# Eight plain gathers ahead of the stored table, joint gathers at most three in flight, and one written-out fill in an attention factorization machine on one core

## What is computed

```python
V = emb_v[x]                                  # (32, 2048, 64)
iu, ju = np.triu_indices(F, k=1)              # 496 pairs
VV = V[iu] * V[ju]
hid = jax.nn.relu(jnp.einsum('pbk,kh->pbh', VV, at_w) + at_b)
score = jnp.einsum('pbh,ho->pbo', hid, at_h)
pooled = jnp.sum(VV * score, axis=0)
at_fm_score = pooled @ p
fm1 = w0 + jnp.sum(w1[x], axis=0)
prob = jax.nn.sigmoid(at_fm_score + fm1)
```

## Time and profile before

| what | value |
|---|---|
| median of 3 runs | 842.64 us (840.57 to 845.03) |
| the profiled execution | 840.11 us, span 838.3 us |
| PE busy | 785.2 us, 94% of the span |
| DVE busy | 721.5 us, 86% |
| ACT busy | 640.2 us, 76% |
| POOL busy | 568.4 us, 68% |
| gathers' share of the 16 DMA engines | 47.1% |

### The profile page before, as it was taken

The page is one execution under the profiler, slowest core; times in us unless marked ns, Lnnn a source line. Parts: engine busy times, 40 slices in busy tenths (PEclk is TensorE's granted clock), DMA queues, the critical chain, the costliest instruction groups (busy, mean ns, idle before and its releaser), DMA issues.

```text
span 838.3 us, 26331 instructions
## 1 busy us (share of the span) xinstructions
PE 785.2 (94%) x10550; PEld 278.0 (33%) x10550; DVE 721.5 (86%) x1221; ACT 640.2 (76%) x672; POOL 568.4 (68%) x553
## 2 busy tenths in 40 slices
PE   0448999999999999999999999999999999999998
PEld 0113333333333333333333333333333333333332
DVE  2473989899999999999999999999999999999884
ACT  0245778788887878888888788898888888888775
POOL 6727767666677666667676666676766667767772
PEclk9878999999999999999999999999999999999999
DMA  9975859635423446543243448823443435833300
GB/s 182 149 47 22 26 23 25 24 23 22 24 21 23 22 21 22 22 22 24 20 24 22 22 21 22 23 22 22 23 23 21 22 21 23 24 21 23 12 1 1
DMA packets 19910, 24.27 MB, mean 29 GB/s; under 512 B 10472, under 2 KB 10541, under 8 KB 19885
## 3 DMA queue, kind: packets, MB, share of 16 engines
q0 software_dynamic: 17408, 17.07, 47.1%
q1 hardware_dynamic: 1535, 6.64, 2.1%
q10 hardware_dynamic: 942, 0.22, 0.1%
HBM read 20.59 MB, written 3.31 MB: 29 GB/s over the span
## 4 chain that ended last, share of the span: by engine, by line
PE 91%; issue 2%; POOL 2%; DMA 2%; ACT 2%; DVE 1%; ACTq 0%
PE Z L580 55%; PE SG L596 27%; PE SG L610 5%; PE Z L544 4%; POOL rows L296 2%; DMA rows<-in_L_rec_emb_v_dram,idx 2%; ACT H L520 1%; ACT pV L465 1%; DVE X L439 0%; DMA idx_raw<-in_r_x_dram 0%; PE Z L674 0%; PE SG L556 0%; ACT V L454 0%; PE Z L653 0%; ACT y_sb L530 0%
## 5 line engine op out<-in xcount | busy, mean ns | idle before, releaser
L439 DVE TENSOR_TENSOR X<-V 128x992 f32<-128x992 f32 (+15 forms) x1024 | 634.8, 691 | 32.5 <-ACT V L454 18.4
L296 POOL DMA_INDIRECT rows<-table,joint_idx x480 | 500.6, 1043 | 232.5 <-issue 153.8
L520 ACT ACTIVATE H<-Z,bias 128x1024 f32<-128x1024 f32 x512 | 529.3, 1119 | 122.8 <-PE Z L580 119.3
L580 PE MATMUL Z<-X,w_sb 64*64 64x512 f32 x4096 | 479.8, 602 | 14.7 <-issue 10.0
L580 PEld LDWEIGHTS Z<-X,w_sb 64*64 64x64 f32 x4096 | 148.2, 132 | 296.3 <-issue 289.3
L596 PE MATMUL SG<-H,score_w 128*32 128x512 f32 x2048 | 239.5, 597 | 0.0
L596 PEld LDWEIGHTS SG<-H,score_w 128*32 128x32 f32 x2048 | 56.8, 109 | 173.7 <-issue 96.1
L465 ACT ACTIVATE pV<-V,pmask 128x1024 f32<-128x1024 f32 x64 | 81.4, 1276 | 0.1
L407 DVE TENSOR_TENSOR prod<-SG,gram 128x512 f32<-128x512 f32 x32 | 22.1, 691 | 61.8 <-PE SG L596 61.8
L454 ACT COPY V<-Z 128x1024 f32<-128x1024 f32 x31 | 31.4, 1012 | 34.7 <-PE Z L544 34.7
L610 PEld LDWEIGHTS SG<-V,pV 128*32 128x32 f32 x4096 | 42.5, 109 | 23.5 <-issue 18.8
(11 more groups left out here) (46 smaller groups left out, 34.5 us busy)
## 6 DMA issues: line engine op xcount, KB each, us to landing
rows<-table,joint_idx POOLq DMA_INDIRECT x480
table<-joined SPq DMA_DIRECT2D x4, 792.0 KB
H<-in_L_rec_emb_v_dram SPq DMA_DIRECT2D x4, 768.0 KB, 8.6
rows<-in_L_rec_emb_v_dram,idx POOLq DMA_INDIRECT x32, 9.0
w_all<-in_L_rec_w_dram,idx POOLq DMA_INDIRECT x32
idx_raw<-in_r_x_dram SPq DMA_DIRECT2D x2, 64.0 KB, 2.0
idx_raw<-in_r_x_dram ACTq DMA_DIRECT2D x2, 64.0 KB, 2.2
table<-tail SPq DMA_DIRECT2D x1, 54.7 KB
```

The lines of the kernel that those rows point to most:

```text
L296: pool.indirect_dma_start(out=rows[t % 2][:, g * FILL_M + m, half, c0:c1], out_offset=None, in_=source, in_offset=bass.IndirectOffsetOnAxi ...
L439: last_one = nc.vector.tensor_tensor(xo, vj, vi.unsqueeze(3).to_broadcast(shape), ALU.mult)
L520: nc.scalar.activation(H[:, s % H_SLOTS, :, COLS * g:COLS * g + COLS], Z[:, z_slot(t, r), :, :], ACT.Relu, bias=bias[:, 0:1]).then_inc(hid ...
L580: done = nc.tensor.matmul(Z[64 * par:64 * par + 64, z_slot(t, r), half, :], w_sb[k, :], X[k, s % X_SLOTS, par, COLS * g:COLS * g + COLS], ...
```

## The change

- Only group 0 of fill 0 is gathered plain (8 gathers instead of 32). Group 1 of fill 0 and all later fills are joint, so they stand behind the wait for the table.
- Every joint gather from fill 1's fourth on waits until the gather three before it has landed. Four semaphores, `rows_landed0` to `rows_landed3`, are used in turn, so that each counts one gather at a time. PE waits for all four ahead of a turn.
- The turn stands ahead of round 6 in every fill that has one in its rounds, but for fill 0, whose order is its own.
- Only fill 0 is written out; the loop begins at fill 1.
- ACT copies `w1` values for fills 0 (group 1) and 1 too; 8 small `w1` gathers are left at the end instead of 32.

```diff
-TURN_BEFORE, LATE_TURN = 6, 12
-LATE_FILLS = (1, 2)
+TURN_BEFORE = 6
...
-PLAIN_FILLS = 2
 TAIL = (VOCAB - MAIN) // TAIL_RUN
 GROUP_AFTER = (0, 3, 7, 10)
+LANES, IN_FLIGHT = 4, 3
...
-def turn_before(t):
-
-    return LATE_TURN if isinstance(t, int) and t in LATE_FILLS else TURN_BEFORE
-
-
-def z_slot(t, r):
-
-    return (r if r < turn_before(t) else r + 1) % Z_SLOTS
+def z_slot(r):
+
+    return (r if r < TURN_BEFORE else r + 1) % Z_SLOTS
...
-        second_rows = sem("second_rows")
-        rows_gathered = [sem(f"rows_gathered{i}") for i in range(2)]
+        rows_landed = [sem(f"rows_landed{lane}") for lane in range(LANES)]
...
         def over_fills(eng, fill):
 
             fill(0, 0, True, False)
-            fill(1, 1, False, False)
-            fill(2, 0, False, False)
-            with eng.Fori(3, FILLS - 2, 2) as t:
+            with eng.Fori(1, FILLS - 2, 2) as t:
                 fill(t, 1, False, False)
                 fill(t + 1, 0, False, False)
             fill(FILLS - 1, (FILLS - 1) % 2, False, True)
...
-            def gather(t, paced=False):
-
-                joint = t >= PLAIN_FILLS
-                source, at_rows = (flat, joint_idx) if joint else (emb_v, idx)
-                for g in range(2):
+            def gather(t, groups=(0, 1), paced=False):
+
+                for g in groups:
+                    joint = t > 0 or g > 0
+                    source, at_rows = (flat, joint_idx) if joint else (emb_v, idx)
                     for m in range(FILL_M):
                         if paced and g == 0 and m == 0:
                             pool.wait_ge(gram_ready, t - 1)
                         elif paced and m % 2 == 0:
                             pool.wait_ge(z_ready, ROUNDS * (t - 2) + GROUP_AFTER[2 * g + m // 2])
                         for half in range(2):
+                            n = GATHERS * (t - 1) + 2 * (FILL_M * g + m) + half
+                            if n >= IN_FLIGHT:
+                                pool.wait_ge(rows_landed[(n - IN_FLIGHT) % LANES], 16 * ((n - IN_FLIGHT) // LANES + 1))
                             col = (2 * half + g) * NM + t * FILL_M + m
                             c0, c1 = (0, ROW) if joint else (EMB_AT[half], EMB_AT[half] + EMB)
-                            arrived = first_rows[g] if t == 0 else second_rows if t == 1 else rows_gathered[t % 2]
+                            arrived = first_rows[g] if t == 0 else rows_landed[n % LANES]
                             pool.indirect_dma_start(out=rows[t % 2][:, g * FILL_M + m, half, c0:c1], out_offset=None,
                                                     in_=source,
                                                     in_offset=bass.IndirectOffsetOnAxis(ap=at_rows[:, col:col + 1], axis=0)
                                                     ).then_inc(arrived, 16)
 
-            plain_w1 = [(Q, n) for n in range(PLAIN_FILLS * FILL_M) for Q in range(QUARTERS)]
+            plain_w1 = [(2 * half, n) for half in range(2) for n in range(FILL_M)]
...
             pool.wait_ge(idx_ready, 1)
-            gather(0)
-            pool.wait_ge(idx_ready, 2)
-            gather(1)
+            gather(0, groups=(0,))
             pool.wait_ge(idx_ready, 4)
             pool.wait_ge(table_stored, 16 * (PIECES + 1))
+            gather(0, groups=(1,))
+            gather(1)
             pool.wait_ge(first_turned, 2)
+            pool.wait_ge(w1_kept, 2)
             gather(2)
             for t in range(3, FILLS):
                 pool.wait_ge(rows_turned, t - 2)
-                pool.wait_ge(w1_kept, 2 * (t - 1 - PLAIN_FILLS))
+                pool.wait_ge(w1_kept, 2 * (t - 1))
                 gather(t, paced=True)
             for Q, n in plain_w1:
                 gather_w1(Q, n)
...
+                g0 = 1 if isinstance(t, int) and t == 0 else 0
                 for half in range(2):
-                    src = rows[parity][:, :, half, W1_AT[half]].rearrange("p (g m) -> p g m", g=2)
-                    nc.scalar.copy(w1_all[:, 2 * half:2 * half + 2, bass.ds(t * FILL_M, FILL_M)], src
+                    src = rows[parity][:, :, half, W1_AT[half]].rearrange("p (g m) -> p g m", g=2)[:, g0:2, :]
+                    nc.scalar.copy(w1_all[:, 2 * half + g0:2 * half + 2, bass.ds(t * FILL_M, FILL_M)], src
                                    ).then_inc(w1_kept, 1)
...
-                        late = turn_before(t) == LATE_TURN
-                        if r == turn_before(t):
+                        if r == TURN_BEFORE:
                             keep_v(t + 1, 1 - parity)
-                        if r == (14 if late else 12):
+                        if r == 12:
                             keep_pv(t + 1, 1 - parity, 0)
                             keep_w1(t + 1, 1 - parity)
-                        if r == (15 if late else 14):
+                        if r == 14:
...
+                        keep_w1(0, 0)
...
                 if first:
                     keep_v(1, 1)
                     for half in range(2):
                         keep_pv(1, 1, half)
+                    keep_w1(1, 1)
...
-                if isinstance(t, int) and t == 1:
-                    pe.wait_ge(second_rows, 16 * GATHERS)
-                else:
-                    pe.wait_ge(rows_gathered[parity], gathered(t, parity))
+                for lane in range(LANES):
+                    pe.wait_ge(rows_landed[lane], 16 * GATHERS // LANES * t)
+                pe.nop(nofuse=True)
...
-                    if r == turn_before(t) and not first and not last:
-                        pe.wait_ge(hid_ready, ROUNDS * t + turn_before(t) - Z_SLOTS + 1)
+                    if r == TURN_BEFORE and not first and not last:
+                        pe.wait_ge(hid_ready, ROUNDS * t + TURN_BEFORE - Z_SLOTS + 1)
                         turn(t + 1, 1 - parity)
...
-                pe.wait_ge(w1_first, 16 * QUARTERS * PLAIN_FILLS * FILL_M)
-                pe.wait_ge(w1_kept, 2 * (FILLS - PLAIN_FILLS))
+                pe.wait_ge(w1_first, 16 * 2 * FILL_M)
+                pe.wait_ge(w1_kept, 2 * FILLS)
                 pe.wait_ge(hid_ready, ROUNDS * FILLS)
...
             products(0, 0, True, False)
-            products(1, 1, False, False)
-            products(2, 0, False, False)
-            products(3, 1, False, False, head)
-            with pe.Fori(3, FILLS - 2, 2) as t:
+            products(1, 1, False, False, head)
+            with pe.Fori(1, FILLS - 2, 2) as t:
                 products(t, 1, False, False, rest)
                 products(t + 1, 0, False, False)
                 products(t + 2, 1, False, False, head)
```

More of the change, by code:

```diff
@@ L92, in z_before @@
         return r - 2
-    return r - 2 if turn_before(t) <= r < turn_before(t) + 2 else r - 3
+    return r - 2 if TURN_BEFORE <= r < TURN_BEFORE + 2 else r - 3
 def afm_kernel(nc, r_x, emb_v, at_w, at_b, at_h, p, w0, w1, out):
@@ L519, in relus @@
                         act.wait_ge(scored, STEPS * t + s - H_SLOTS + 1)
[L520 removed]
+                    nc.scalar.activation(H[:, s % H_SLOTS, :, COLS * g:COLS * g + COLS], Z[:, z_slot(r), :, :], ACT.Relu,
                                          bias=bias[:, 0:1]).then_inc(hid_ready, 1)
@@ L569, in hidden @@
                 pe.wait_ge(x_ready, ROUNDS * t + r + 1)
-                if r == turn_before(t) + 2 and not first and not last:
+                if r == TURN_BEFORE + 2 and not first and not last:
                     pe.wait_ge(v_ready, t + 1)
                 elif not first or r >= Z_SLOTS:
-                    pe.wait_ge(hid_ready, ROUNDS * t + z_before(t, r) + 1)
+                    pe.wait_ge(hid_ready, ROUNDS * t + z_before(r) + 1)
                 pe.nop(nofuse=True)
@@ L579, in hidden @@
                     for par in range(2):
-                        done = nc.tensor.matmul(Z[64 * par:64 * par + 64, z_slot(t, r), half, :], w_sb[k, :],
+                        done = nc.tensor.matmul(Z[64 * par:64 * par + 64, z_slot(r), half, :], w_sb[k, :],
                                                 X[k, s % X_SLOTS, par, COLS * g:COLS * g + COLS], start=True, stop=True)
```

5 lines of the change are left out of this document (1 added, 4 removed).

## The result

The changed kernel took **888.98 us** at the median of its four runs (873.7, 881.0, 896.95 and 908.95), beside 841.84 for the kernel before on the same chip, 5.6% more. Executions more than 1.5% above a kernel's quickest count as slow and are left out of every ratio here, so the ratio of 1.042, 95% interval 1.033 to 1.051, rests on the two quickest runs alone. It is slower, and even the quickest run lies above the range of 835 to 859. The profiled execution is that quickest one, 873.7 us; its span of 871.8 us is **33.5 us** longer than the 838.3 of before.

What follows compares the result with a forecast made beforehand. TensorE's own work was taken as the bound, 24.08 us a fill. Terms +1.3 (start), -0.2 (loop), +1.3 (middle), -0.5 (end) sum to +1.9, on the median of 842.64 giving 844.5 us, range 835 to 859.

Steps and rivals of the forecast that it cites:

- Steps 1 and 2: Start: table stored by 32 us instead of 64; first joint gather at 32.8, fill 2's last rows landing at 90.1.
- the pace of 1.41: Gather stream: with three in flight, one gather every 1.41 us, with ends 1.25 and 1.60.
- Rival A: Gather stream: the cap doesn't bind, POOL keeps its own pace, 4.6 us go; 837.5 us, chance 0.26.
- Step 3: PE through fills 0 and 1: waits 8.6 us for fill 2's rows; fill 2's grams at 108.5, +1.3 us.
- The stop of 8 us: PE's 8.32 us issue stop at 54.3 in fill 0, read as late code behind gathers; expected to go.
- my 3.0: Start: PE's clock at 0.50 after the idle wait before fill 2's transposes, 3.0 us lost.
- Step 4: Loop from fill 1: fill 2's grams to fill 5's take 73.17 us instead of 73.41, -0.2 us.
- Step 6: End: eight w1 gathers instead of 32, hidden; only fill 31's grams lose their neighbour, 1.86 to 1.30, -0.5 us.
- Step 5: Middle: nothing on PE waits; the last gather reaches slightly into the grams, 0.05 x 27 fills, +1.3 us.
- Rival C: Middle: gathers run over the grams in every fill, 0.55 us each, 15 us in all; 858 us, chance 0.12.
- Rival B: Middle: POOL becomes the slower bound, beyond 1.505 us per gather; at 1.55, 869 us; chance 0.12.

Runs made afterwards that it cites:

- f1_no_cap: The changed kernel without its landing waits, gathers counted on two semaphores again: 841.23 us beside 837.66 for the kernel before, ratio 1.0049.
- g2: Kernel before with its late turns, only 8 plain gathers, joint gathers without a cap; on a slow chip 1113.39 us beside 1121.49.
- g4: Kernel before with a wait on PE's round ahead of every gather from fill 3 on, no landing waits; slow chip, 1070.86 us beside 1121.49.
- h2: Kernel before with its late turns, only 8 plain gathers, joint gathers without a cap; on a slow chip 1111.17 us beside 1121.04.
- h3: Kernel before with GpSimd's wait on the grams left out; on a slow chip 1092.95 us beside 1121.04.
- i2_late_stream: Kernel before with its late turns, only 8 plain gathers, joint gathers without a cap: 842.15 us, ratio 1.0047 to the kernel before.
- j1_turn9: Changed kernel without its landing waits, transposes of every fill at round 9 instead of 6: 840.26 us, ratio 1.0045 to the kernel before.
- f2_before_capped: Kernel before plus the three-in-flight wait with four semaphores from fill 2 on, nothing else: 893.72 us beside 837.66.

## Why the prediction was wrong

*Steps 1 and 2.* First joint gather 33.9 (32.8): right. Last rows of fill 2 at 93.7 (90.1): the pace of 1.41 was about right, but I let the first eleven gathers go at 1.25. POOL issues them so, and the first eight land 1.43 us apart (37.13 to 47.16). Rival A falls with that: without the cap the rows come at 92.0, where 4.6 us less than 90.1 would be 85.5.

*Step 3.* The stop of 8 us is gone, fill 1's transposes at 70.96 (68.2), PE stands still 8.42 us (8.6). Fill 2's grams +3.7 instead of +1.3. The clock cost less than my 3.0: the transposes took 1.94 for 1.09 and the 48 products 6.44 for 5.54, 1.8 together. That a short queue of gathers lets the code in was not shown; f1_no_cap has a longer one and no such stop.

*Step 4* can't be read in the changed kernel apart from the grams' loss. In f1_no_cap, which has the same loop, fill 2's grams to fill 5's take 72.24 us (110.03 to 182.27) against 73.41 before: -1.2, where I had -0.2. *Step 6* was right, -0.5. Without the cap the parts of its profile come to start +2.9, middle -1.3 and end -0.6, +1.0 us of span.

*Step 5, the middle, is the step that failed.* I took +1.3 with ends 0 and 15; it was **+30.4**. Two errors lie in it. The smaller one: I saw that the last gather would end 0.7 us after the grams begin, had the price of 0.55 us from the end of the trace, and averaged it to 0.05, because one pair of grams at the start had shown only 0.10. What counts is not that a gather runs beside the grams but that one starts inside them; then it is 0.55 nearly each time, and with 20 such fills of 29 it came to 10.4 us. Rival C had the mechanism and the price of a hit right; its 15 us took every fill as hit.

The larger error: I asked what the wait costs POOL (a gather of 1.56 us, a pace, a reserve) and concluded that PE never waits. A single gather of 14 us doesn't appear in a pace. One that is 13 us late stops PE, because the next transposes want its rows. Rival B named the contention with VectorE, but as a slower pace in every fill; it came as two single gathers.

The trace had a row on which I dismissed it, and one that spoke against that, the gather of 2.84 us above. I wrote that back-to-back gathers stand beside the X products at 0.94 us. That is true of nearly all back-to-back gathers, and the cap turned many of them into gathers that come from a wait. In the changed kernel 146 of the 520 gathers had idle time of more than 0.31 us before them, in the kernel before 34 of 544. In all traces without the extra write, of the gathers that began in a gapless run with 1.8 us or more of it left, 56 of 381 with such idle time took over 2.5 us, and 5 of 3400 without.

What stays open: why a gather behind a wait is shut out so much more often than those 0.30 us apart (the five of these were all on slow chips, four of 9.7 us and one of 14.56, in g2, g4, h2 and h3); why only two of 146 were hit in the changed kernel; by what path a starting gather makes PE pause; and what sets 1.41 us a gather.

## What to carry to other kernels

A wait added to a queue "that has slack" changes when its instructions start, not only how many fit: look at what the other engines are doing at those moments, and count the worst single case, not the pace. Keep GpSimd's gathers back to back, or give VectorE's runs of two-operand products a break as often as a gather may come, and don't let gathers start inside a burst of small matmuls. And when an experiment gains in one place, look one fill further: in i2_late_stream the code stop came back, and in j1_turn9, whose fill 2 came 2.2 us sooner than in f1_no_cap, fill 31's grams stood only 0.1 us sooner.

## What the runs showed of the hardware that I had not expected

- A single 128-row gather on POOL took 14.2 us instead of 0.94 while VectorE ran 24 products of two SBUF operands without a break, and ended 0.81 us behind the run. A write without a source, 59 ns once a round, prevented it altogether.
- A gather that starts inside a series of 128 small matmuls makes them last about 1.85 us instead of 1.30; one that started 0.44 us or more before them costs nothing (576.87 in the changed kernel: 1.30 us beside the 14.16 us gather). In f2_before_capped two that started 0.24 and 0.40 us before them cost 0.24.
- Chips differ by a third on the same program, 838 and 1121 us, with PE waiting far more often for instructions on the slow ones. There, the kernel before without its gram wait was 2.5 to 5% *faster* than the kernel before, and 1.4% slower where that takes 838, so a slow chip can turn a verdict round.
